# Expert slots filled by an indirect DMA through memory in place of one-hot matmuls, in a Flamingo-style block with a mixture of experts

## The reference

```
xt = layernorm(x).reshape(448, 256)
scores = sqrt(softplus(xt @ gate_w.T))
_, idx = top_k(scores + gate_b, 2)
w = take(scores, idx); w = w / sum(w)
pos = place of each pair (token, expert) in its expert's list, in token order
valid = pos < 128
buf[e, pos] = token's row of xt                 # 16 x 128 x 256
h = silu(buf @ W1.T) * (buf @ W3.T)             # 176 wide
out = h @ W2.T
y = sum over the two experts of out[e, pos] * w * valid
shared = (silu(xt @ Ws1.T) * (xt @ Ws3.T)) @ Ws2.T
x = x + tanh(g_ffn) * (y + shared)
```

## Time and profile before

| | us |
|---|---|
| median of 3 runs | 411.51 |
| lowest, highest of them | 406.88, 412.04 |
| span of the profiled execution | 405.0 |
| PE, DVE, ACT, POOL busy in it | 358.6, 303.5, 250.9, 124.1 |

### The profile page before, as it was taken

How to read it: one execution, slowest core, us unless ns; L and a number is a source line. 1 busy time by engine, 2 the same in 40 slices (tenths; PEclk the granted TensorE clock), 3 DMA queues, 4 the chain that set the end, 5 groups by cost and what they waited for, 6 DMA issues and landing times.

```text
span 405.0 us, 14019 instructions
## 1 busy us (share of the span) xinstructions
PE 358.6 (89%) x5793; PEld 269.3 (67%) x5793; DVE 303.5 (75%) x656; ACT 250.9 (62%) x412; POOL 124.1 (31%) x116
## 2 busy tenths in 40 slices
PE   0896899999998998998999999998864699999993
PEld 0663468668677766855866776786643587888882
DVE  3888886775776676586577668668896877999993
ACT  3476477777686676776768666567721535666761
POOL 6151462132022122222203300001101054787870
PEclk9999699999999999999999999999985858999998
DMA  7869965565294186166336208544000009635001
GB/s 253 196 157 197 241 146 134 87 159 136 58 171 115 53 152 182 54 106 175 103 61 125 54 14 142 129 137 141 3 2 2 1 1 306 191 116 163 2 0 45
DMA packets 34512, 45.65 MB, mean 113 GB/s; under 512 B 3995, under 2 KB 30299, under 8 KB 34323
## 3 DMA queue, kind: packets, MB, share of 16 engines
q1 hardware_dynamic: 33395, 43.74, 44.5%
q0 software_dynamic: 640, 0.78, 0.9%
q10 hardware_dynamic: 416, 0.26, 0.3%
HBM read 25.08 MB, written 0.47 MB: 63 GB/s over the span
## 4 chain that ended last, share of the span: by engine, by line
PE 76%; DVE 13%; issue 5%; ACT 2%; POOL 2%; DMA 1%; DVEq 0%; ACTq 0%; POOLq 0%
PE PS L1035 35%; PE PS L1101 9%; PE PS L1078 8%; PE PS L1112 7%; PE PS L1363 4%; PE PS L1322 3%; DVE mx L794 2%; PE PS L1088 2%; PE PS L1346 2%; PE PS L1312 1%; DMA x_in<-x 1%; DVE KN L743 1%; PE PS L1279 1%; DVE st L697 1%; DVE mtop L798 1%
## 5 line engine op out<-in xcount | busy, mean ns | idle before, releaser
L794 DVE TENSOR_REDUCE mx<-PS 112x1 f32<-112x500 f32 (+1 forms) x128 | 114.3, 933 | 52.8 <-PE PS L1078 52.7
L501 ACT ACTIVATE PT_all<-PS 128x1344 f32<-128x1344 f32 x64 | 82.6, 1290 | 10.1 <-PE PS L1101 9.9
L1035 PE MATMUL PS<-cT,wkvT 128*128 128x500 f16 x288 | 71.5, 385 | 18.0 <-POOL slot_of L404 11.2
L1035 PE MATMUL PS<-wkvT,cT 128*125 128x256 f16 x576 | 73.2, 279 | 0.0
L1035 PEld LDWEIGHTS PS<-wkvT,cT 128*125 128x125 f16 x576 | 65.3, 139 | 5.3 <-issue 0.5
L395 POOL TENSOR_TENSOR cT<-c_in,cT 128x1000 f16<-128x1000 f32 x18 | 37.5, 2082 | 86.9 <-ACT cT L479 86.9
L1035 PEld LDWEIGHTS PS<-cT,wkvT 128*128 128x128 f16 x288 | 27.5, 99 | 50.8 <-POOL slot_of L404 11.2
L486 ACT ACTIVATE KN<-PS,col_in 128x500 f16<-128x500 f32 x48 | 32.5, 677 | 40.6 <-PE PS L1035 40.6
L1078 PE MATMUL PS<-arena,QC 96*112 96x500 f16 x192 | 52.4, 380 | 3.1 <-issue 2.8
L1101 PE MATMUL PS<-QC,arena 98*128 98x112 f16 x768 | 49.2, 214 | 3.0 <-ACT QC L521 2.9
L493 ACT ACTIVATE V<-PS 125x512 f32<-125x512 f32 x48 | 28.7, 598 | 30.6 <-PE PS L1035 30.6
(11 more groups left out here) (207 smaller groups left out, 463.8 us busy)
## 6 DMA issues: line engine op xcount, KB each, us to landing
arena<-KN SPq DMA_DIRECT2D x144, 125.0 KB, 3.6
c_in<-ctx SPq DMA_DIRECT2D x24, 500.0 KB, 4.5
cT<-W SPq DMA_DIRECT2D x11, 352.0 KB
c_in<-W SPq DMA_DIRECT2D x6, 352.0 KB
cT<-W SPq DMA_DIRECT2D x11, 176.0 KB
arena<-place_far SPq DMA_DIRECT2D x1, 1568.0 KB, 10.0
c_in<-W SPq DMA_DIRECT2D x6, 176.0 KB
PT_all<-L_xattn_wkv SPq DMA_DIRECT2D x1, 512.0 KB, 6.1
```

The lines of the kernel that those rows point to most:

```text
L501: act.activation(PT_all[:, u % 4, :].rearrange("p (c k) -> p c k", c=CH), PS[:, 3:6, 0:4 * TP], ACT.Exp, scale=SCORE).then_inc(s["exp_done ...
L794: dve.tensor_reduce(mx[:, u % 2, k:k + 1], PS[0:TP, k:1 + k * (CH - 1), 0:CW], AX.XY, ALU.max).then_inc(s["red_done"], 1)
L1035: ins = mm(out_, w(a, h), x_(b, h), start=first and k == 0, stop=last and k == len(todo) - 1)
```

## The change

Each token now has a row of 1092 bytes in SBUF (`x_row`): the high and the low half of its 256 numbers, its number (1 to 448), and its 16 weights. When the row numbers (expert x 128 + place) are known (`rows_at`), POOL issues 8 indirect DMAs (2 choices x 4 tiles, 112 rows each) that write the rows to their slots in memory (`rows_far`, which SP has filled with zeros during the attention by 4 DMAs of 560 KB). SP waits for all 8 and reads the slots back in 5 DMAs, of 1, 1, 2, 4 and 8 experts (`LOADS`, `slot_rows`). `gather` and `weigh_slots` become `turn_rows`, 4 transposes of float16 data; `select` and `slot_weights` fall away; `turned_select` compares the slot's token number with 448 token numbers made once; `place_far` and its three DMAs fall away.

The order changes too: DVE finishes the router before `hidden(1)` and the low halves `hT` of the shared expert, PE counts the places before both results of the shared expert; the halves of weights 1 and 2 are made earlier; and in the loop of the experts `tokens_hi`, `w13_hi` and `w2_hi` (ACT) and `w13_lo` (DVE) stand behind the tanh and the hidden rows, one expert further ahead.

```diff
 KW = 1504
 QR = 3 * PW
+RW = 2 * D + 2 + 2 * E
+TOKEN, WEIGHT = D, D + 1
...
-        slot_of = sb("slot_of", [128, 1])
-        place_far = nc.dram_tensor("place_far", (E * TT, TP), F16, kind="Internal").ap()
+        token16 = over_keys(128, T)
+        slot_rows = over_keys(CAP, E, RW)
+        slot_rows32 = slot_rows.bitcast(F32)
+        rows_far = nc.dram_tensor("rows_far", (E * CAP, RW // 2), F32, kind="Internal").ap()
         PS = stack.enter_context(nc.psum_tensor("PS", [128, 8, 512], F32))
...
                     stack_keys(b + 1, 1, c)
                     if b + 3 < B:
                         load_context(b + 3, c)
+                if b < 4:
+                    need(sp, "consts", NCONST)
+                    sp.dma_start(rows_far[4 * b * CAP:4 * (b + 1) * CAP].rearrange("(e c) w -> c e w", c=CAP),
+                                 zero_row[:].bitcast(F32).unsqueeze(1).to_broadcast([CAP, 4, RW // 2])).then_inc(s["rows_zero"], 16)
             def load_weights(j):
...
                 load_weights(j)
-            sp.wait_ge(s["place_copied"], 1)
-            sp.dma_start(place_far, placeT[:]).then_inc(s["place_out"], 16)
-            sp.wait_ge(s["place_out"], 16)
-            far = place_far.rearrange("r p -> (r p)").partition_broadcast(128)
-            sp.dma_start(place_row[:, 0:2].rearrange("p e t -> p (e t)"), far[:, 0:2 * T]).then_inc(s["place_in0"], 16)
-            sp.dma_start(place_row[:, 2:E].rearrange("p e t -> p (e t)"), far[:, 2 * T:E * T]).then_inc(s["place_in1"], 16)
+            sp.wait_ge(s["rows_out"], 16 * 2 * TT)
+            for k, (a, b) in enumerate(LOADS):
+                sp.dma_start(slot_rows32[:, a:b], rows_far[a * CAP:b * CAP].rearrange("(e c) w -> c e w", c=CAP)).then_inc(rows_in[k], 16)
             for j in range(NW, E + 1):
...
                 gp.tensor_tensor(rstd[:, part], var[:, part], mhalf[:, part], ALU.pow).then_inc(s["rstd_ready"], 1)
-            gp.wait_ge(s["act_post"], 4)
-            gp.tensor_tensor(x16[:, :, 1], xn[:], x16[:, :, 0], ALU.subtract).then_inc(s["x16_ready"], 1)
-            for j in range(1, E + 1):
+            gp.wait_ge(s["x_halved"], 1)
+            gp.iota(token16, [[1, T]], base=1, channel_multiplier=0, allow_small_or_imprecise_dtypes=True).then_inc(s["tokens_ready"], 1)
+            gp.iota(x_row32[:, :, TOKEN:TOKEN + 1], [[TP, TT], [0, 1]], base=1, channel_multiplier=1,
+                    allow_small_or_imprecise_dtypes=True).then_inc(s["tokens_ready"], 1)
+            gp.tensor_tensor(x_row[:, :, D:2 * D], xn[:], x_row[:, :, 0:D], ALU.subtract).then_inc(s["x_halved"], 1)
+            need(gp, "w2l_done", 1)
+            w2_lo(1)
+            gp.wait_ge(s["x_halved"], 2)
+            gp.wait_ge(s["tokens_ready"], 2)
+            gp.wait_ge(s["rows_zero"], 16 * 4)
+            gp.wait_ge(s["rows_ready"], 1)
+            gp.wait_ge(s["places_ready"], 1)
+            for k in range(2):
+                for t in range(TT):
+                    gp.indirect_dma_start(out=rows_far, out_offset=bass.IndirectOffsetOnAxis(ap=rows_at[:, k, t:t + 1], axis=0),
+                                          in_=x_row32[:, t, :], in_offset=None, bounds_check=E * CAP - 1,
+                                          oob_is_err=False).then_inc(s["rows_out"], 16)
+            for j in range(2, E + 1):
                 need(gp, "w2l_done", j)
                 w2_lo(j)
...
                 act.wait_ge(s["lnt_done"], k + 1)
                 act.activation(xT[:, :, part], turned[k], ACT.Copy).then_inc(s["lnc_done"], 1)
                 act.activation(xT16[:, 0, :, part], turned[k], ACT.Copy).then_inc(s["xh_done"], 1)
+            w13_hi(1)
+            act.activation(x_row[:, :, 0:D], xn[:], ACT.Copy).then_inc(s["x_halved"], 1)
+            w2_hi(1)
...
-            act.activation(x16[:, :, 0], xn[:], ACT.Copy).then_inc(s["act_post"], 1)
...
-            w2_hi(1)
-            w13_hi(1)
...
             def expert(e):
                 if e > 0:
                     result_hi(e - 1)
-                if e + 1 < E:
-                    w13_hi(e + 2)
-                    tokens_hi(e + 1)
                 need(act, "ht_ready", e + 1)
                 act.activation(heT[:, 0, :], PS[0:IH, turn_bank, 0:2 * CAP], ACT.Copy).then_inc(s["hh_done"], 1)
                 if e + 1 < E:
-                    if e > 0:
-                        w2_hi(e + 2)
                     hidden_tanh(e + 1)
+                if e + 2 < E:
+                    tokens_hi(e + 2)
+                    w13_hi(e + 3)
+                if 0 < e < E - 1:
+                    w2_hi(e + 2)
+            w13_hi(2)
...
+            w2_hi(2)
             tokens_hi(0)
-            w2_hi(2)
             hidden_tanh(0)
+            tokens_hi(1)
...
@@ -893,7 +918,7 @@
             dve.tensor_tensor(xT16[:, 1, :, 0:3 * TP], xT[:, :, 0:3 * TP], xT16[:, 0, :, 0:3 * TP], ALU.subtract).then_inc(s["xl_done"], 1)
             dve.wait_ge(s["xh_done"], 2)
             post(dve.tensor_tensor(xT16[:, 1, :, 3 * TP:T], xT[:, :, 3 * TP:T], xT16[:, 0, :, 3 * TP:T], ALU.subtract))
+            w13_lo(1)
...
-                    one(dve.scalar_tensor_tensor(bias[:], oh[:], -3e38, bias[:], ALU.mult, ALU.add))
-                    hidden(1)
-                if k == 1:
-                    one(dve.tensor_tensor(c_[:], e_[:], z[:], ALU.add))
-                    post(dve.tensor_copy(sel16[:], c_[:]))
-                dve.wait_ge(s["shared_hh"], k + 1)
-                dve.tensor_tensor(hT[:, 1, k, :], PS[0:IH, h_bank[k], 0:4 * TP], hT[:, 0, k, :], ALU.subtract).then_inc(s["shared_hl"], 1)
+                    one(dve.scalar_tensor_tensor(bias[:], oh, -3e38, bias[:], ALU.mult, ALU.add))
+            one(dve.tensor_tensor(c_[:], picked[:, 0], picked[:, 1], ALU.add))
+            post(dve.tensor_copy(sel16[:], c_[:]))
...
-            d.did(dve.tensor_tensor(wt16[:, :, :, 1], a[:], wt16[:, :, :, 0], ALU.subtract))
+            dve.tensor_tensor(x_row32[:, :, WEIGHT:WEIGHT + E], a[:], rs[1][:].unsqueeze(2).to_broadcast([TP, TT, E]),
+                              ALU.mult).then_inc(s["rows_ready"], 1)
+            counts = PS[0:TP, place_bank, 0:TT * E].rearrange("p (t e) -> p t e", t=TT)
             dve.wait_ge(s["pe_post"], 4)
-            one(dve.scalar_tensor_tensor(b_[:], PS[0:TP, place_bank, 0:TT * E].rearrange("p (t e) -> p t e", t=TT), 1.0, c_[:], ALU.add, ALU.mult))
-            post(dve.tensor_scalar(place[:].rearrange("p (e t) -> p t e", t=TT), b_[:], -1.0, None, ALU.add))
+            one(dve.tensor_tensor(b_[:], counts, ends[:], ALU.is_ge))
+            one(dve.scalar_tensor_tensor(b_[:], b_[:], FAR, counts, ALU.mult, ALU.add))
+            one(dve.tensor_tensor(placed[:], picked[:], b_[:].unsqueeze(1).to_broadcast([TP, 2, TT, E]), ALU.mult))
+            with nc.allow_low_precision(reason="row numbers: one whole number and zeros"):
+                dve.tensor_reduce(rows_at[:], placed[:], AX.X, ALU.add).then_inc(s["places_ready"], 1)
+            for p in range(2):
+                if p == 1:
+                    hidden(1)
+                dve.wait_ge(s["shared_hh"], p + 1)
+                dve.tensor_tensor(hT[:, 1, p, :], PS[0:IH, h_bank[p], 0:4 * TP], hT[:, 0, p, :], ALU.subtract).then_inc(s["shared_hl"], 1)
...
             def turned_select(e):
-                if e == 0:
-                    dve.wait_ge(s["place_in0"], 16)
-                elif e == 2:
-                    dve.wait_ge(s["place_in1"], 16)
                 need(dve, "added", e - 1)
-                dve.tensor_scalar(selT[e % 2], place_row[:, e, :], slot_of[:, 0:1], None, ALU.is_equal).then_inc(s["st_done"], 1)
-            def slot_weights(e):
-                need(dve, "st_ready", e + 1)
-                need(dve, "h_done", e)
-                dve.tensor_scalar(slot_w[:], PS[:, sum_bank, 0:1], PS[:, sum_bank, 1:2], 0.5 / FS,
-                                  ALU.add, ALU.mult).then_inc(s["slot_w_done"], 1)
+                dve.tensor_tensor(selT[e % 2], token16, slot_rows32[:, e, TOKEN:TOKEN + 1].to_broadcast([CAP, T]),
+                                  ALU.is_equal).then_inc(s["st_done"], 1)
...
-                need(dve, "slot_w_done", e + 1)
-                dve.scalar_tensor_tensor(hn_e[e % 2], PS[:, gu_bank, I:2 * I], slot_w[:, 0:1], hg_e, ALU.mult, ALU.mult).then_inc(s["h_done"], 1)
...
             def expert(e):
                 if e > 0:
                     result_lo(e - 1)
-                if e + 1 < E:
-                    w13_lo(e + 2)
                 need(dve, "hh_done", e + 1)
                 dve.tensor_tensor(heT[:, 1, :], PS[0:IH, turn_bank, 0:2 * CAP], heT[:, 0, :], ALU.subtract).then_inc(s["hl_done"], 1)
-                if e + 2 < E:
-                    select(e + 2)
-                if e + 1 < E:
-                    slot_weights(e + 1)
                 turned_select(e)
                 if e + 1 < E:
                     hidden_rows(e + 1)
-            dve.wait_ge(s["dve_post"], 5)
-            select(0)
-            select(1)
```

(44 more changed lines are left out.)

77 lines of the change are left out of this document (34 added, 43 removed).

## The result

The changed kernel takes 417.06 us (median of 4 runs, 413.77 to 419.01), the kernel before 410.66 beside it (4 runs): a ratio of **1.0177 [1.0102, 1.0253]**. The medians themselves differ by 6.4 us. The kernel is slower beyond the noise; whether by more than 2% these runs leave open. The profiled execution took 419.01 us, with a span of 416.0.

What follows compares the result with a forecast made beforehand. PE, busy 89% of the span, was taken as the bound before, the ring in the changed loop. 11.4 + 0.8 - 5.1 + 0.2 = +7.3 us, span 412.3; the median lies 6.5 above: 418.8 us, range 409 to 426.

Steps and rivals of the forecast that it cites:

- The ring: Expert loop: gates_and_ups, tanh, tokens, w13_hi and w13_lo wait on one another in a circle, setting a 3.52 us pitch.
- Rival A: Expert loop: the ring is slack, PE or POOL sets a 3.1 us pitch; +1.8, 413.3 us; 13%.
- PE's own 3.03: Expert loop: pitch if PE stays the bound, 3.95 - 1.14 + 0.22 = 3.03 us.
- Rival D: Expert loop: w2_lo's subtraction and w13_lo exclude one another, pitch 3.75 us; +10.3, 421.8 us; 10%.
- The router: Before the scatter: new order worth 3.5 us, POOL takes back 2.9; places near 329.3, hardly earlier than before.
- Rival E: Router: not ahead at all, POOL blocking every step; places at 331, +9, 420.5 us; inside the forecast's own range, which has 55%.
- The scatter: Row numbers to slots in memory: eight indirect DMAs at 1.1 us each, 8.8 us (4.6 to 17), plus 2.4 to land.
- The read back: After the scatter: first load of slots, 140 KB, takes 3.6 us plus 0.1; slots there at 344.2.
- B (dear): Scatter: 1.6 us an issue gives +11.3, 422.8 us; 2.13 gives +15.5, 427; 15%.
- C (cheap): Scatter cheap and hidden: issue at 0.57, no lock on the router, pitch 3.03 us; -6.2, 405.3 us; 7%.
- At nothing: Items priced at 0, chiefly the four fills of zeros during the attention (between 0 and +2 us).
- The end: After the last experts: the last W2 half may come a little late, +0.2 us.

Runs made afterwards that it cites:

- e1_ring: Changed kernel with ACT making w13_hi(e + 3) before the tanh of e + 1: 409.86 us, ratio 0.9988 to the kernel before.
- e5_both: Changed kernel with w13_hi before the tanh, POOL's subtraction and w2_lo(1) out of the router's time, DVE's turned select behind w13_lo: 414.83 us, ratio 1.0128.
- e3_fills: Changed kernel with the four fills of zeros made three times, the other two into spare memory: 418.86 us, ratio 1.0228.
- e9_order: e5_both with DVE's turned select of e moved back ahead of the hidden rows of e + 1: 408.0 us, ratio 0.9932.
- e10_hybrid_order: e5_both with experts 0 to 3 gathered by one-hot matmuls, and the turned select ahead of the hidden rows again: 401.56 us, ratio 0.9747.

## Why the prediction came out right

**The place of the gain and of the loss.** Forecast were +11.4 at the start, +0.8 to expert 2, -5.1 in thirteen pitches, +0.2 at the end, +7.3 in all. Measured from the logits: 33.99 - 22.65 = +11.3, 7.79 - 7.26 = +0.5, 46.38 - 50.87 = -4.5, +0.65, in all +8.0 in the profiles and +7.3 by the ratio. The time itself, forecast at 418.8 us (409 to 426), came out at 417.06.

**The ring** was priced at 3.52 and takes 3.585. Its pieces, start to start, with the forecast in brackets: gates and ups 1.10 (1.09), tanh 0.22 (0.22; ACT's row has the tokens' copy from 386.76), tokens 0.50 (0.47), w13_hi 0.81 (0.81), w13_lo and the hand-over to PE 0.95 (0.93). Rival A (a slack ring, 3.1) is refuted by e1_ring: 3.084 is what comes once it is open. PE's own 3.03 was priced 0.05 low. Rival D (the lock holds the loop) did not happen in the changed kernel: the turned select is held there too (L992, 0.91 us at 385.96 against 0.61), but it stands off the ring, and DVE still waits 0.41 us for w13_hi behind it. Once the ring is open, the lock is one line away: e5_both has 3.637, where D forecast 3.75, though what is held there is the turned select and not w13_lo.

**The router.** Row numbers 0.6 us earlier than before, as forecast (329.3 against 329.9). The order by itself gives 15.21 - 12.00 = 3.2 (forecast 3.5), POOL takes back 2.6 (forecast 2.9). The held operations were L927 and L936, ahead of and behind the one that I named (L907 before, L932 after); the sum was near since whichever stands there waits for the subtraction's end. The rule that the prediction took from "SBUF — State Buffer" of the Trainium skill, section "SBUF: two separate sides", that the two exclude one another for the whole instruction, agrees with the trace for POOL's subtraction; for its one-input operation it does not: L934 took its usual 0.22 us beside L456. Rival E (331) is out: 332.23 - 2.94 = 329.3.

**The scatter** is where two sizes were off and cancelled. From row numbers to the last landing I took 8 x 1.1 + 2.4 = 11.2 us; it was 344.85 - 332.23 = 12.6. An issue holds POOL 0.94 to 1.08 us, as taken, but there is 0.30 between two (1.25 to 1.39 from start to start), and 0.98 between row numbers and the first; the last landing ends 2.60 after the start of its issue where I had 3.5. The read back took 2.2 (344.85 to 347.03) and not 3.7. Slots there: 347.03 - 2.94 = 344.1, forecast 344.2. The way through memory so took as long as forecast, between the rivals B (dear) and C (cheap). That the estimate lay there was luck in part, and that its two errors cancelled was luck: the trace of before bounded an issue only between 0.57 and 2.13.

**At nothing:** the fills, by e3_fills to within a microsecond or so. **The end** was 0.65, not 0.2; the half of W2 that I named was not looked into, and it is open.

**The sum against the runs.** From one execution to the next the copy of the logits moves by several us. Without it as a mark, 2.94 us would have been given to the scatter.

## What to carry to other kernels

A detour through memory is a fixed delay, here some 15 us from row numbers to the first slots; in e9_order, where nothing covers it, it ate 31.40 - 22.65 = 8.8 of the 50.87 - 39.93 = 10.9 us that the shorter pitches gave; in e10_hybrid_order, where the first four experts take the old road, it ate none. When steps of a software pipeline are moved behind one another, follow one item round from engine to engine: if it comes back to the start one turn later, the pitch can't be less than the sum of its pieces, though no engine is full. And an order that is free on one engine may be dear beside another that shares its port: compare the duration of the moved operation before and after, not its place alone.
